# Skipping far key blocks by ALiBi slope in the attention loop, and alternating buffers in the first normalisation, in an eight-core pre-norm layer kernel

## Reference

```python
q = apply_rope((ln(x) @ Wq) heads)      # 16 heads of 128
k, v = ...                              # 4 KV heads, repeated 4 times
scores = q @ k.T / sqrt(128)
dist = minimum(pos_k - pos_q, 0)
slopes = 2.0 ** (-8.0 * arange(1, 17) / 16)
scores = scores + slopes[h] * dist      # ALiBi
scores = where(pos_k > pos_q, -inf, scores)
x = x + (softmax(scores) @ v) @ Wo
# FFN on ln(x): softmax gate over 64, top 8, eight groups g:
#   xg = x + soft @ mask_up;  d = down(silu(gate(xg)) * up(xg));  y += scalar_g * d
```

## Time and profile before

| what | us |
|---|---|
| median of the runs (two: 3681.76 and 3688.08) | 3684.92 |
| the profiled execution | 3672.09 |
| its span on the slowest core, core 3 | 3669.9 |
| spans of the eight cores | 3657.8 to 3669.9 |
| TensorE busy (matmuls) | 3145.0 |
| DVE, ACT, POOL busy | 1094.5, 424.8, 385.0 |

### The profile page before, as it was taken

How to read it: one execution, slowest core, us unless ns; L and a number is a source line. 1 busy time by engine, 2 the same in 40 slices (tenths; PEclk the granted TensorE clock), 3 DMA queues, 4 the chain that set the end, 5 groups by cost and what they waited for, 6 DMA issues and landing times.

```text
span 3669.9 us, 34912 instructions; the slowest of 8 cores (3657.8 to 3669.9 us)
## 1 busy us (share of the span) xinstructions
PE 3145.0 (86%) x12866; PEld 1338.3 (36%) x12866; DVE 1094.5 (30%) x1395; ACT 424.8 (12%) x650; POOL 385.0 (10%) x350
## 2 busy tenths in 40 slices
PE   1247787789888689879999999999999999999986
PEld 1222332122222344724344344343443443443434
DVE  3542144433333211541321412313213214123123
ACT  1210012333333311000000000000000000000000
POOL 0000010000000010011111111111111111111110
PEclk9998897555555689579999999999999999999998
DMA  4221263000000163067667677677676676676755
GB/s 112 77 52 18 23 59 42 1 1 1 1 1 12 52 84 31 0 71 73 68 67 75 63 69 70 62 77 69 63 74 67 66 77 63 68 73 60 74 51 119
DMA packets 640663, 200.70 MB, mean 55 GB/s; under 512 B 632034, under 2 KB 632547, under 8 KB 639220
## 3 DMA queue, kind: packets, MB, share of 16 engines
q0 software_dynamic: 628208, 159.67, 45.1%
q1 hardware_dynamic: 12292, 38.82, 3.4%
HBM read 349.72 MB, written 8.39 MB: 98 GB/s over the span
## 4 chain that ended last, share of the span: by engine, by line
PE 77%; DVE 9%; DMA 7%; issue 4%; ACT 2%; DVEq 0%; SPq 0%; ACTq 0%; POOLq 0%
PE PS L1149 17%; PE PS L1155 17%; PE PS L1200 13%; DMA AR<-downT 4%; PE PS L710 4%; PE PS L671 3%; PE PS L502 3%; PE PS L715 3%; PE PS L667 3%; DVE AR L721 2%; PE PS L811 2%; PE PS L398 2%; PE PS L453 2%; PE PS L356 2%; DMA AR<-x_perm 2%
## 5 line engine op out<-in xcount | busy, mean ns | idle before, releaser
L1149 PE MATMUL PS<-AR 128*128 128x512 bf16 x2816 | 841.2, 380 | 16.8 <-DVE AR L1116 16.8
L1155 PE MATMUL PS<-AR 128*128 128x512 bf16 x2816 | 840.9, 380 | 0.0
L1200 PE MATMUL PS<-AR 128*128 128x512 bf16 x2816 | 639.2, 383 | 32.0 <-DMA AR<-downT 23.1
L1200 PEld LDWEIGHTS PS<-AR 128*128 128x128 bf16 x2816 | 268.6, 98 | 407.6 <-issue 111.2
L1174 DVE TENSOR_TENSOR AR<-PS,AR 128x1024 bf16<-128x1024 f32 x88 | 107.8, 1225 | 1026.1 <-ACT AR L1169 1026.1
L1149 PEld LDWEIGHTS PS<-AR 128*128 128x128 bf16 x2816 | 275.7, 98 | 353.6 <-issue 25.0
L1155 PEld LDWEIGHTS PS<-AR 128*128 128x128 bf16 x2816 | 276.4, 98 | 334.8 <-issue 4.4
L1169 ACT ACTIVATE AR<-PS 128x1024 bf16<-128x1024 f32 x88 | 90.1, 1024 | 1822.2 <-PE PS L1155 1822.2
L1212 DVE TENSOR_TENSOR AR<-AR,PS 128x1024 f32<-128x1024 f32 x128 | 156.3, 1221 | 443.9 <-PE PS L1200 437.2
L690 ACT ACTIVATE AR<-PS,AR 128x512 bf16<-128x512 f32 (+3 forms) x384 | 221.3, 580 | 429.0 <-PE PS L671 302.4
L710 PE MATMUL PS<-AR 128*128 128x512 bf16 (+3 forms) x384 | 188.1, 490 | 79.9 <-DVE AR L698 79.3
(11 more groups left out here) (121 smaller groups left out, 1835.3 us busy)
## 6 DMA issues: line engine op xcount, KB each, us to landing
AR<-gateT POOLq DMA_DIRECT2D x88, 512.0 KB, 6.4
AR<-upT POOLq DMA_DIRECT2D x88, 512.0 KB, 8.3
AR<-downT POOLq DMA_DIRECT2D x128, 352.0 KB, 5.2
AR<-x_perm SPq DMA_DIRECT2D x48, 512.0 KB, 4.0
AR<-Wq POOLq DMA_DIRECT2D x16, 512.0 KB, 8.1
AR<-Wo POOLq DMA_DIRECT2D x16, 512.0 KB, 6.5
out<-AR SPq DMA_DIRECT2D x8, 1024.0 KB, 3.9
AR<-Wk POOLq DMA_DIRECT2D x4, 512.0 KB, 8.2
```

What stands on the lines that cost most here:

```text
L1149: fn = (lambda t_, hh=hh, tc=tc, psG=psG, sl=sg: nc.tensor.matmul(psG[:, tc * 512:(tc + 1) * 512], GSL[sl][:, hh * 128:(hh + 1) * 128], XG ...
L1155: fn = (lambda t_, hh=hh, tc=tc, psU=psU, sl=su: nc.tensor.matmul(psU[:, tc * 512:(tc + 1) * 512], USL[sl][:, hh * 128:(hh + 1) * 128], XG ...
L1200: fn = (lambda t_, it=it, tc=tc, psD=psD, sl=sd: nc.tensor.matmul(psD[:, tc * 512:(tc + 1) * 512], DSL[sl][:, it * 128:(it + 1) * 128], AP ...
```

## The change

There are two edits.

The first adds `_active_tiles(h, gq)`, which goes through `SCHED[gq]` and keeps a tile only if the head's slope times the least distance between its keys and the unit's leading queries is below 150. The attention loop takes its list from there. The tile's slot in the mask table is carried along; `sl4` is counted by the tile's place in the shortened list.

The second makes the first normalisation alternate by the parity of tt: two `XLNORM` buffers (the second on the place of `WSL[1]`, which is not in use yet), two sets of statistics columns, and the last value of each semaphore token kept for each parity. EPS moves from column 12 to column 62.

```diff
+_SLOPES = 2.0 ** (-8.0 * np.arange(1, NH + 1) / NH)
+
+def _active_tiles(h, gq):
+    base = 4 * gq
+    out = []
+    for kind, kp, s, slot in SCHED[gq]:
+        jlead = base + s
+        if kind == "own":
+            dmin = 256 * (jlead - kp) - 127
+        else:
+            dmin = 256 * (jlead - (kp - 8)) - 255
+        if _SLOPES[h] * max(dmin, 0) < 150.0:
+            out.append((kind, kp, s, slot))
+    return out
...
-    XLNORM = f32v(192512, 1024)
+    XLNORMP = [f32v(192512, 1024), f32v(196608, 1024)]
...
     for tt in range(16):
+        par = tt % 2
...
-            p.wait("ve", "VE", prev_rtok)
-            rtok = p.inc("ve", lambda v, s=slot, c=(cS0, cS1)[hc]: v.reduce_sum(
-                out=scr(c), in_=XL[s], axis=AX.X), "VE")
-            prev_rtok = rtok
+            p.wait("ve", "VE", prev_rtok[par])
+            rtok = p.inc("ve", lambda v, s=slot, par=par, c=(cS0, cS1)[hc]: v.reduce_sum(
+                out=scrp(c, par), in_=XL[s], axis=AX.X), "VE")
+            prev_rtok[par] = rtok
...
-            p.wait("ve", "TE", te_norm_free)
-            p.wait("ve", "VE", prev_nv_tok)
-            nv_tok = p.inc("ve", lambda v, sl=slot: v.tensor_scalar(
-                out=XLNORM, in0=XL[sl], scalar1=scr(cR), scalar2=scr(cNMR),
+            p.wait("ve", "TE", te_norm_free[par])
+            p.wait("ve", "VE", prev_nv_tok[par])
+            nv_tok = p.inc("ve", lambda v, sl=slot, par=par: v.tensor_scalar(
+                out=XLNORMP[par], in0=XL[sl], scalar1=scrp(cR, par), scalar2=scrp(cNMR, par),
                 op0=ALU.mult, op1=ALU.add), "VE")
...
-            p.wait("ve", "TE", te_norm_free)
+            p.wait("ve", "TE", te_norm_free[par])
...
-            sched = SCHED[gq]
+            sched = _active_tiles(h, gq)
```

More of the change, by code:

```diff
@@ L274, in build @@
     se_xl_free = [0, 0]
-    te_norm_free = 0
-    cS0, cS1, cQ0, cQ1, cSUM, cSQ, cM, cMSQ, cVAR, cR, cNMR, cTMP, cEPS = range(13)
+    te_norm_free = [0, 0]
+    cS0, cS1, cQ0, cQ1, cSUM, cSQ, cM, cMSQ, cVAR, cR, cNMR, cTMP = range(12)
+    cEPS = 62
     def scr(col):
@@ L284, in build @@
     p.wait("te", "LD", ldc)
[L285 to L289, removed]
+    p.emit("ve", lambda v: v.memset(SCR[:, 62:63], EPS))
+    prev_ve_tok = [0, 0]
+    prev_sq_tok = [0, 0]
+    prev_rtok = [0, 0]
+    prev_nv_tok = [0, 0]
     tpose_done = []
@@ L293, in build, with scr, scrp @@
     for tt in range(16):
+        par = tt % 2
+        def scr(col, par=None, _S=SCR):
+            return _S[:, col:col + 1]
+        def scrp(col, par):
+            return SCR[:, 16 * par + col:16 * par + col + 1]
         for hc in (0, 1):
@@ L301, in build @@
             p.wait("ve", *xld[tt * 2 + hc])
-            p.wait("ve", "VE", prev_rtok)
-            rtok = p.inc("ve", lambda v, s=slot, c=(cS0, cS1)[hc]: v.reduce_sum(
-                out=scr(c), in_=XL[s], axis=AX.X), "VE")
-            prev_rtok = rtok
+            p.wait("ve", "VE", prev_rtok[par])
+            rtok = p.inc("ve", lambda v, s=slot, par=par, c=(cS0, cS1)[hc]: v.reduce_sum(
+                out=scrp(c, par), in_=XL[s], axis=AX.X), "VE")
+            prev_rtok[par] = rtok
             p.wait("se", *xld[tt * 2 + hc])
-            p.wait("se", "VE", prev_ve_tok)
@@ L308, in build @@
[L308 to L311, removed]
+            p.wait("se", "VE", prev_ve_tok[par])
+            p.wait("se", "SE", prev_sq_tok[par])
+            sq_tok = p.inc("se", lambda s_, sl=slot, par=par, c=(cQ0, cQ1)[hc]: s_.activation(
+                HJUNK, XL[sl], AF.Square, accum_out=scrp(c, par)), "SE")
@@ L312, in build @@
+            prev_sq_tok[par] = sq_tok
         p.wait("ve", "VE", rtok)
-        t1 = p.inc("ve", lambda v: v.tensor_tensor(
-            out=scr(cSUM), in0=scr(cS0), in1=scr(cS1), op=ALU.add), "VE")
+        t1 = p.inc("ve", lambda v, par=par: v.tensor_tensor(
+            out=scrp(cSUM, par), in0=scrp(cS0, par), in1=scrp(cS1, par), op=ALU.add), "VE")
         p.wait("ve", "SE", sq_tok)
-        t2 = p.inc("ve", lambda v: v.tensor_tensor(
-            out=scr(cSQ), in0=scr(cQ0), in1=scr(cQ1), op=ALU.add), "VE")
+        t2 = p.inc("ve", lambda v, par=par: v.tensor_tensor(
+            out=scrp(cSQ, par), in0=scrp(cQ0, par), in1=scrp(cQ1, par), op=ALU.add), "VE")
@@ L318, in build @@
         p.wait("ve", "VE", t1)
-        t3 = p.inc("ve", lambda v: v.tensor_scalar(out=scr(cM), in0=scr(cSUM),
+        t3 = p.inc("ve", lambda v, par=par: v.tensor_scalar(out=scrp(cM, par), in0=scrp(cSUM, par),
                    scalar1=1.0 / D, scalar2=None, op0=ALU.mult), "VE")
         p.wait("ve", "VE", t3)
-        t4 = p.inc("ve", lambda v: v.tensor_scalar(out=scr(cMSQ), in0=scr(cM),
-                   scalar1=scr(cM), scalar2=None, op0=ALU.mult), "VE")
+        t4 = p.inc("ve", lambda v, par=par: v.tensor_scalar(out=scrp(cMSQ, par), in0=scrp(cM, par),
+                   scalar1=scrp(cM, par), scalar2=None, op0=ALU.mult), "VE")
@@ L324, in build @@
         p.wait("ve", "VE", t4)
-        ve_tok = p.inc("ve", lambda v: v.scalar_tensor_tensor(
-            out=scr(cVAR), in0=scr(cSQ), scalar=1.0 / D, in1=scr(cMSQ),
+        ve_tok = p.inc("ve", lambda v, par=par: v.scalar_tensor_tensor(
+            out=scrp(cVAR, par), in0=scrp(cSQ, par), scalar=1.0 / D, in1=scrp(cMSQ, par),
             op0=ALU.mult, op1=ALU.subtract), "VE")
-        prev_ve_tok = ve_tok
+        prev_ve_tok[par] = ve_tok
         p.wait("se", "VE", ve_tok)
-        s1 = p.inc("se", lambda s_: s_.activation(scr(cTMP), scr(cVAR), AF.Ln,
+        s1 = p.inc("se", lambda s_, par=par: s_.activation(scrp(cTMP, par), scrp(cVAR, par), AF.Ln,
@@ L331, in build @@
                    bias=scr(cEPS)), "SE")
         p.wait("se", "SE", s1)
-        se_tok = p.inc("se", lambda s_: s_.activation(scr(cR), scr(cTMP), AF.Exp,
+        se_tok = p.inc("se", lambda s_, par=par: s_.activation(scrp(cR, par), scrp(cTMP, par), AF.Exp,
                        scale=-0.5), "SE")
         p.wait("ve", "SE", se_tok)
-        ve_tok = p.inc("ve", lambda v: v.tensor_scalar(
-            out=scr(cNMR), in0=scr(cM), scalar1=scr(cR), scalar2=-1.0,
+        ve_tok = p.inc("ve", lambda v, par=par: v.tensor_scalar(
+            out=scrp(cNMR, par), in0=scrp(cM, par), scalar1=scrp(cR, par), scalar2=-1.0,
@@ L343, in build @@
             se_xl_free[slot] = se_tok
-            p.wait("ve", "TE", te_norm_free)
-            p.wait("ve", "VE", prev_nv_tok)
-            nv_tok = p.inc("ve", lambda v, sl=slot: v.tensor_scalar(
-                out=XLNORM, in0=XL[sl], scalar1=scr(cR), scalar2=scr(cNMR),
+            p.wait("ve", "TE", te_norm_free[par])
+            p.wait("ve", "VE", prev_nv_tok[par])
+            nv_tok = p.inc("ve", lambda v, sl=slot, par=par: v.tensor_scalar(
+                out=XLNORMP[par], in0=XL[sl], scalar1=scrp(cR, par), scalar2=scrp(cNMR, par),
                 op0=ALU.mult, op1=ALU.add), "VE")
-            prev_nv_tok = nv_tok
+            prev_nv_tok[par] = nv_tok
             ve_xl_free[slot] = nv_tok
@@ L355, in build @@
             for j in range(8):
-                fn = (lambda t_, j=j, ps=ps, sl=slot: nc.tensor.transpose(
+                fn = (lambda t_, j=j, ps=ps, par=par: nc.tensor.transpose(
                     ps[:, j * 128:(j + 1) * 128],
-                    XLNORM[:, j * 128:(j + 1) * 128], IDNF))
+                    XLNORMP[par][:, j * 128:(j + 1) * 128], IDNF))
                 if j == 7:
-                    te_norm_free = p.inc("te", fn, "TE")
+                    te_norm_free[par] = p.inc("te", fn, "TE")
                 else:
                     p.emit("te", fn)
-            p.wait("ve", "TE", te_norm_free)
+            p.wait("ve", "TE", te_norm_free[par])
             ev = p.inc("ve", lambda v, ps=ps, hc=hc, tt=tt: v.tensor_copy(
@@ L856, in build_p3 @@
     p.wait("se", "VE", t3)
-    s1 = p.inc("se", lambda s_: s_.activation(RSTD, VTMP, AF.Ln, bias=SCR[:, 12:13]), "SE")
+    s1 = p.inc("se", lambda s_: s_.activation(RSTD, VTMP, AF.Ln, bias=SCR[:, 62:63]), "SE")
     p.wait("se", "SE", s1)
```

## The result

| | before | after |
|---|---|---|
| median of the runs | 3684.92 us (2 runs) | 3657.85 us (27 runs) |
| ratio after to before, runs on the same chip | | 0.9899, 95% interval 0.9873 to 0.9925 |
| profiled execution, slowest core | 3672.1, core 3 | 3649.4, core 0 |
| its span | 3669.9 | 3647.7 |

The changed kernel is 1.0% faster, and the interval leaves no change out. In us that is 0.0101 x 3684.9 = 37 (28 to 47 by the interval), where 34.9 were forecast. The two medians come from different sets of runs, so I go by the ratio, which compares runs on the same chip.

What follows compares the result with a forecast made beforehand. TensorE bounds the kernel; in attention heads 0 to 3 it alternates with an ACT and DVE chain. Tiles save 34.9 us, buffers and slots 0, lifts unchanged: 3684.9 - 34.9 = 3650 us, range 3636 to 3664.

Steps and rivals of the forecast that it cites:

- lift: Attention: a short rise of TensorE's granted clock that shortens a unit; one more or less on the slowest core is 7.7 us.
- The two floors: Shortened gq=1 units, heads 0 to 3: each takes the larger of two lower bounds; with head 4, 34.9 us saved.
- the chain's floor: Attention, ACT and DVE: the gq=0 unit, 15.47 us, plus 1.49 us for each full tile left beyond its eight.
- TensorE's: Attention, lower bound by TensorE: today's unit of gq=1 minus 1.92 us for each tile taken.
- so this counts as no difference: Whole kernel: 0.9% less lies under the about 2% a measurement can tell; 0.97 for within 2%.
- the rival with a lift lost: Attention, slowest core: 27.2 us saved in place of 34.9; chance 0.17, shared with chain's price or ring wait.
- The first normalisation: First stage, second edit: alternating buffers cost 0, from -73.6 us to +1 us or so; the stage keeps its length.
- The rival in which the buffers hide the wait: First stage: normalisation runs under the transposes; half of DVE's wait gives 3613 us, all 3576; chance 0.02.
- The ring of four slots: Attention, start of units after shortened ones: reusing score and PSB slots out of step adds 0, at most 13 us.
- the uncovered wait: Attention, unit starts: without cover three score pairs come late in four units, 4 x 3.3 = 13 us; taken as 0.
- a change in heads 5 to 15 other than by lifts: Attention, later heads: a sign that the prediction is wrong; no size given.
- The slower rival: FFN: more matmuls at the low clock; 205 undo the gain, 640 give 3759 us; chance 0.03, two thirds short of 2%.

Runs made afterwards that it cites:

- e1: The kernel before with the first edit alone (19 tiles left out); ratio to the kernel before 0.9922.
- e10: The first edit alone on the kernel before, measured again beside the changed kernel on the same chip; ratio to the kernel before 0.9896.
- e3: The kernel before with the mask product of tile i put behind the clamp of tile i+1 on DVE; ratio to the kernel before 0.9965.
- e4: The changed kernel with the bound 30 in place of 150, so 51 tiles go in place of 19; ratio to the kernel before 0.9751.
- e7: The kernel before, all 384 tiles, with the ALiBi matmul on 128 rows in place of one; ratio to the kernel before 0.9653.
- e11: The changed kernel with both edits, measured again beside its two halves on the same chip; ratio to the kernel before 0.9899.
- e2: The changed kernel with all 384 tiles, so the second edit alone; ratio to the kernel before 0.9981.
- e5: The changed kernel with the ALiBi matmul made with 128 rows, 127 of them zero, in place of one; ratio to the kernel before 0.9564.
- e9: The second edit alone, all tiles in place, measured again in five rounds; ratio to the kernel before 0.9981.

## Why the prediction was right or wrong

**The size.** Forecast 3650 us, 34.9 us less; measured 37 us less by the ratio, which makes 3648 of the 3684.9. (The median of 3657.85 in the table is not to be set against the forecast, for the reason given beside it.) On cores without a lift the attention went from 632.6 + 7.7 = 640.3 us (core 3 before, its one lift added back) to 606.6 (cores 0, 5 and 7 after): 33.7 us. The two floors gave 34.9. Heads 0 and 1 came out 0.3 and 0.4 us over the chain's floor, by one late instruction each, whose cause is open. Head 3 came out 0.4 us under TensorE's, and in e1 and e10, where the attention is the same, it takes from 22.9 us, the chain's floor, to 23.3: the price of 1.92 us for a tile was somewhat too low for it. e3, e4 and e7 show each floor by itself. That the ratio gives 37 us and the like cores 33.7 is within the interval.

**The step that failed: "so this counts as no difference".** The sum had 34.9 us, and I set the bound for telling it from nothing at 2%, 74 us, took that bound from no row, and gave 0.97 to a time within it. The difference is clear: the interval of the ratio is 0.0052 wide, 19 us, and it leaves 1 out by far (0.9873 to 0.9925, and 0.9879 to 0.9919 in e11). The price of the tiles was right; what was mis-sized is the noise it was set against. A forecast of 0.9% less should have been called a small gain.

**Lifts.** The prediction left open which units would be lifted and took the slowest core's share as it was. Over the eight cores of the profiled executions the attention fell by 26.6 us on average (627.7 to 601.0), 7 us less than on cores without a lift: lifts gave 12.6 us per core before and 5.6 after. That is the size and the sign of the rival with a lift lost, and e1 looks the same (600.3 us on average). The runs do not show such a loss. The one profile of the kernel before is of a short execution: 3672.1 us, where each of the 26 runs beside the changed kernel took 3674.17 or more, and its cores' spans average 3662.6 us, where they average 3670.0 over the runs beside e11. The changed kernel has 3635.7 in its profile and 3633.4 over its runs in e11, so over the runs the cores gained 36.6 us. The 7 us of lifts are about what that one execution was short by; that the kernel before usually has fewer lifts than in it is likely, but no profile of a usual execution is there to show it. The same must be kept in mind for e2 and e3, whose profiles are set against it above.

The prediction cited the Trainium skill, "TensorE: Matmul & The Clock Gate", Part 1, What's actually happening, for a clock that is throttled by default and released by activity. It drew from this that lifts become rarer with fewer matmuls, and that is not borne out: e4, with 51 tiles gone, has 8.3 us of lifts per core where the changed kernel has 5.6, and in e5 TensorE is busy for a smaller share and has the higher clock. What made the difference in e5 is what kind of matmul it does.

**The first normalisation** was costed at 0 from the order of the instructions, and its length and DVE's wait say 0. The rival in which the buffers hide the wait is refuted (e2, e9). With all tiles in place the edit is worth 0.2% by another way, which stays open; on top of the tiles no gain shows.

**The ring of four slots** was costed at 0. No unit of gq=0 that follows a shortened one is longer by more than 0.3 us, and that 0.3 appears in the unit of head 3 in the changed kernel, which follows 12 tiles and so starts on the same slot as ever, and in heads 2 and 3 in e10, where the attention is the same. After the 13 tiles of head 3 and the 15 of head 4 nothing is added (12.5 us). So the 0.3 moves with the program and not with the ring, and it is far from the 3.3 us of the uncovered wait. The zero stands. The prediction had named a change in heads 5 to 15 other than by lifts as a sign of being wrong; head 13's 0.3 us, absent from e1 and e10, is one, small and open.

**The slower rival**, the clock of the FFN, did not come: 0.97 as before. The 3.7 us more in 2110 compare two different cores; over all eight, what follows the last reciprocal takes 2425.7 us on average, where it took 2425.5.

## What to carry to other kernels

Where two limits take turns, price a removed piece from units that are made of the same pieces, and take the larger of the floors for what is left: that held within 0.6 us per unit of heads 0 to 4 in the changed kernel, and of those that e4 and e7 were run for. A gain under the size that one execution can show is still a gain: say its sign and ask for the interval. One profiled execution can be 7 us off its kernel's usual time, so a difference of that size between two profiles needs the spans of many runs beside it. And where a busy TensorE has a low granted clock, look first at what its matmuls are: one narrow matmul in four cost this kernel more than the 19 tiles did.

## What the runs showed of the hardware

- Taking the ALiBi matmul over 128 rows, 127 of them zero, in place of one row, with the same columns, moved the granted clock of heads 4 to 15 from 0.54 to 0.86 and the kernel from a ratio of 0.990 to 0.956 (e5); e7 has the same with all tiles (0.85 to 0.86 over the cores, 0.54 to 0.56 before). Zero operands did not keep the clock low.
- Changing between 128 rows and one costs start-to-start time at both levels, for 512 columns: 0.56 and 0.53 us against 0.40 and 0.43 at 1.2 GHz, and 0.32 against 0.22 at 2.4 GHz (kernel before); with 128 rows in both it is 0.22 (e5). Whether it lies in the matmul or in its weight load was not separated.
- The second edit alone, a few waits and addresses in the first stage, made the kernel 0.2% faster in two measurements with that stage at its old length (e2, e9). Where the 0.2% lies is not shown.
